# Four graph layers on one core: one table for maximum and sum, a later hold, wide passes in pieces, and a division moved behind the block builder

## The reference, cut to what matters

```python
# first layer: attention over a node's incoming edges
e = leaky_relu(concat(h[src], h[dst], rel[type]) @ attn_w1 @ attn_w2, 0.01)
ex = exp(e - segment_max(e, dst)[dst])
a = ex / segment_sum(ex, dst)[dst]
h_new = where(deg > 0, segment_sum(a * h[src], dst), h); relu(h_new + h @ loop_weight)
# second layer: sum of messages; then two rounds of weighted averaging
# last layer: 8 heads, the edges and a loop at every node
e = a_src[src] + a_dst[dst]; e = where(e > 0, e, 0.2 * e)
e = exp(e - segment_max(e, dst)[dst])
alpha = e / (segment_sum(e, dst)[dst] + 1e-16)
out = segment_sum(alpha * (h @ W_att)[src], dst).mean(heads) + bias
# then two layer norms with a feed-forward block between them
```

## Time and profile before

| | us |
|---|---|
| median of 3 executions | 3177.5 (3170.21 to 3187.55) |
| profiled execution, its own time | 3182.19 |
| its span | 3180.5 |
| busy: TensorE, VectorE, GpSimd, ScalarE | 2093.6, 1963.4, 1061.6, 551.9 |

### The profile page before, as it was taken

How to read it: one execution, slowest core, us unless ns; L and a number is a source line. 1 busy time by engine, 2 the same in 40 slices (tenths; PEclk the granted TensorE clock), 3 DMA queues, 4 the chain that set the end, 5 groups by cost and what they waited for, 6 DMA issues and landing times.

```text
span 3180.5 us, 45724 instructions
## 1 busy us (share of the span) xinstructions
PE 2093.6 (66%) x15154; PEld 1599.8 (50%) x15155; DVE 1963.4 (62%) x3088; ACT 551.9 (17%) x1123; POOL 1061.6 (33%) x984
## 2 busy tenths in 40 slices
PE   0426881699999879979995777774016777614463
PEld 0411221588887779953334666664015666514462
DVE  6789996888898720040104999999935555502274
ACT  0000001344454414410001222221030000000010
POOL 1014002400000000000003777774867777877300
PEclk9655885899999959989997999998558999955575
DMA  2034331233333425548772221220173343212440
GB/s 74 1 80 103 119 100 26 85 144 143 156 161 161 174 95 181 189 176 297 265 289 53 52 52 39 82 52 21 34 252 104 87 124 89 49 25 76 55 88 10
DMA packets 157367, 346.89 MB, mean 109 GB/s; under 512 B 67016, under 2 KB 81523, under 8 KB 150037
## 3 DMA queue, kind: packets, MB, share of 16 engines
q1 hardware_dynamic: 88677, 169.61, 15.8%
q10 hardware_dynamic: 36560, 141.07, 12.5%
q0 software_dynamic: 32032, 34.94, 5.9%
HBM read 220.22 MB, written 124.90 MB: 109 GB/s over the span
## 4 chain that ended last, share of the span: by engine, by line
PE 30%; DVE 24%; POOL 19%; issue 15%; DVEq 3%; DMA 1%; ACT 1%; SPq 0%; POOLq 0%; ACTq 0%
POOL ring L681 16%; PE PS L1226 8%; DVE big L1827 5%; PE PS L1190 4%; PE PS L1261 3%; DVE big L1947 3%; PE PS L1198 2%; PE PS L1251 2%; DVE big L1941 2%; DVE s_ring L1676 2%; PE PS L1073 2%; PE PS L1067 1%; DVE big L1823 1%; DVE s_ring L1670 1%; POOL nmx L687 1%
## 5 line engine op out<-in xcount | busy, mean ns | idle before, releaser
L681 POOL DMA_INDIRECT ring<-d_h,idx_lin x784 | 836.2, 1067 | 848.4 <-DMA d_h<-Hn 557.4
L1306 PEld LDWEIGHTS PS<-arena,s_ring 128*128 128x128 f32 x1968 | 316.1, 212 | 21.9 <-issue 0.4
L1306 PE MATMUL PS<-arena,s_ring 128*128 x1968 | 304.8, 282 | 0.0
L1827 DVE TENSOR_TENSOR big<-big,qa 128x900 bf16<-128x900 bf16 x525 | 296.9, 622 | 0.0
L1122 PE MATMUL PS<-big,qa 128*128 128x225 bf16 x1050 | 262.3, 266 | 38.2 <-DVE big L1827 37.4
L1226 PE MATMUL PS<-big,arena 125*64 125x500 f32 (+1 forms) x700 | 270.4, 546 | 25.8 <-DVEq L1362 25.8
L1999 DVE TENSOR_TENSOR big<-big,PS 128x512 f32 x123 | 84.5, 687 | 321.6 <-PE PS L1306 319.7
L1125 PE MATMUL PS<-big,qa 128*128 128x150 bf16 x2100 | 268.7, 233 | 0.0
L1261 PE MATMUL PS<-big,arena 125*128 125x200 bf16 x2352 | 238.4, 252 | 0.4 <-ACT arena L908 0.4
L1302 PE MATMUL PS<-zero_bf 128*128 128x512 bf16 x123 | 51.0, 415 | 270.8 <-ACTq L949 123.5
L1251 PE MATMUL PS<-big 128*125 128x128 bf16 x784 | 133.0, 293 | 129.5 <-DVE big L1941 125.2
(11 more groups left out here) (446 smaller groups left out, 3629.7 us busy)
## 6 DMA issues: line engine op xcount, KB each, us to landing
big<-d_blk SPq DMA_DIRECT2D x24, 2000.0 KB, 7.6
d_blk<-big ACTq DMA_DIRECT2D x13, 3125.0 KB, 9.2
big<-d_blk SPq DMA_DIRECT2D x25, 1562.5 KB, 6.3
d_blk<-arena ACTq DMA_DIRECT2D x12, 3125.0 KB, 9.2
big<-d_blk SPq DMA_DIRECT2D x12, 2250.0 KB, 8.1
d_stash<-ring SPq DMA_DIRECT2D x98, 256.0 KB, 2.0
arena<-d_stash ACTq DMA_DIRECT2D x98, 256.0 KB, 2.7
ring<-d_h,idx_lin POOLq DMA_INDIRECT x784
```

The costliest lines, as they stand in the source:

```text
L681: pool.indirect_dma_start(ring[:, HALF * h + s, :], None, table, bass.IndirectOffsetOnAxis(ap=idx_lin[:, CH * i + s:CH * i + s + 1], axis= ...
L1306: mm = nc.tensor.matmul(PS[:, bass.ds(place[s] + j % SUMS * BANK, D)], marks[:, j % 2, s, :], arena[:, bass.ds(at[s], D)], start=False, st ...
L1827: last = v_.tensor_tensor(pair_c(half, p, 1, 6, 1), pair_c(half, p, 0, 6, 0), at_wa[:, :, :, bass.ds(k + 2 * p, 2)], ALU.mult)
```

## The change

- **Last layer, one table.** Maximum and sum stand side by side in `big`, 16 values an edge, and are written together to `d_top3`. One group of 25 reads brings both to the nodes (`ntop`), in place of two groups. The column stride of both is 64 bytes. The zeroing of the accumulator stands behind this one write. The write of the maxima ahead of exp is gone.
- **The hold** stands behind 44 chunks (40 before), the alpha rows behind 54 (50).
- **Wide passes** are cut in four pieces each, issued one behind the other.
- **First layer.** The exponentials are written to `d_al0` as they are. The backward fill of the sum, the reciprocal and the product are gone; the forward sums are written to `d_sum0`, and 25 more reads bring them to the nodes (`tot0`, 1 for nodes without edges), behind those of `norm`. Behind the last block, VectorE takes their reciprocal and multiplies `agg_sb` by it. ScalarE's first block waits for the write, since it overwrites the sums.
- Helpers (`col`, `scan_heads`, `row_carry`) now take an array with its stride and offset; `node_terms` and the copies of the escape factors use `ntop`.

```diff
-        FILL_AT, LOOK_AT, ROWS_AT, NODES_AT = 24, 40, 50, 84
+        FILL_AT, LOOK_AT, ROWS_AT, NODES_AT = 24, 44, 54, 84
...
+            sp.wait_ge(S["exp_done"], 1)
+            sp.dma_start(d_al0.rearrange("(p c) k -> p (c k)", p=P), qa[:, 0:C]).then_inc(S["alpha_out"], 16)
             sp.wait_ge(S["alpha_ready"], 1)
-            sp.dma_start(d_al0.rearrange("(p c) k -> p (c k)", p=P), qa[:, 0:C]).then_inc(S["alpha_out"], 16)
+            sp.dma_start(d_sum0.rearrange("(p c) k -> p (c k)", p=P), arena[:, C:2 * C]).then_inc(S["codes_out"], 16)
...
             node_rows(d_wsum, free(norm[:, 0:1], [[1, NB], [1, 1]]), last_i)
+            pool.wait_ge(S["codes_out"], 16 * 8)
+            node_rows(d_sum0, free(tot0[:, 0:1], [[1, NB], [1, 1]]), last_i)
...
-            pool.wait_ge(S["nmx_ready"], 1)
-            pool.wait_ge(S["max_out"], 16)
-            node_rows(d_max3, packed(nmx, H), last_i)
+            pool.wait_ge(S["ntop_ready"], 1)
             pool.wait_ge(S["scan_out"], 16)
-            node_rows(d_sum3, packed(nsum, H), last_i)
+            node_rows(d_top3, ntop, last_i)
             tiles(d_h3, NODES_AT, NCH)
...
             act.wait_ge(S["dense_ready"], 1)
+            act.wait_ge(S["codes_out"], 16 * 8)
             block_out(None, 0, True)
...
             act.wait_ge(S["exp_in"], 2)
-            act.dma_start(d_max3.rearrange("(p c) k -> p (c k)", p=P), big[:, 0:W3]).then_inc(S["max_out"], 16)
             nc.scalar.activation(qa[:, 0:W3], qa[:, 0:W3], ACT.Exp).then_inc(S["exp_done"], 1)
...
             act.wait_ge(S["scan_ready"], 2)
-            act.dma_start(d_sum3.rearrange("(p c) k -> p (c k)", p=P), big[:, W3:2 * W3]).then_inc(S["scan_out"], 16)
-            act.wait_ge(S["max_out"], 16)
-            for j in range(W3 // BANK):
-                nc.scalar.activation(acc[:, j * BANK:(j + 1) * BANK], zero_bf[:], ACT.Copy)
+            act.dma_start(d_top3.rearrange("(p c) k -> p (c k)", p=P), big[:, 0:2 * W3]).then_inc(S["scan_out"], 16)
             act.wait_ge(S["scan_out"], 16)
-            for j in range(W3 // BANK, NB * HD // BANK):
+            for j in range(NB * HD // BANK):
                 last = nc.scalar.activation(acc[:, j * BANK:(j + 1) * BANK], zero_bf[:], ACT.Copy)
...
-            for back in (0, 0, 1, 0, 1):
+            for back in (0, 0, 1, 0):
                 chain(1, back)
...
             go(v_.memset(norm[:], 0.0))
+            go(v_.memset(tot0[:], 1.0))
...
                 scan_one(q, b1, notst, cf_sum, SUMOP, 0.0)
-                scan_one(b1, b2, notst, cb_sum, FILLOP, 0.0, 1)
-                go(v_.reciprocal(b0, b2))
-                go(v_.tensor_tensor(q, q, b0, ALU.mult))
                 mark("alpha_ready")
...
+            def col(b, j):
+
+                return free(b[0][:, 0:1], [[b[1], C]], b[2] + j)
+
+            def wide(b, k):
+
+                return free(b[0][:, 0:1], [[b[1], C // 4], [1, H]], b[2] + k * C // 4 * b[1])
...
-                q, sm, total = qa[:, 0:W3], big[:, 0:W3], big[:, W3:2 * W3]
+                q, sm, total = (qa[:, 0:W3], H, 0), (big[:, 0:2 * W3], 2 * H, 0), (big[:, 0:2 * W3], 2 * H, H)
+
+                def combine(op):
+
+                    for k in range(4):
+                        go(v_.tensor_tensor(wide(q, k), wide(q, k), wide(sm, k), op), False)
+                    v.wait_ge(S["dve"], done[0])
...
-                row_carry(sm, cf_sum, SUMOP, 0.0, 0, lambda: v_.tensor_tensor(q, q, sm, ALU.add))
+                row_carry(sm, cf_sum, SUMOP, 0.0, 0, lambda: combine(ALU.add))
...
-                go(v_.scalar_tensor_tensor(q, q, slope, q, ALU.mult, ALU.max))
+                for k in range(4):
+                    go(v_.scalar_tensor_tensor(wide(q, k), wide(q, k), slope, wide(q, k), ALU.mult, ALU.max), False)
+                v.wait_ge(S["dve"], done[0])
...
-                go(v_.tensor_tensor(q, q, sm, ALU.subtract))
+                combine(ALU.subtract)
                 mark("exp_in")
...
+            v.wait_ge(S["nodes_in"], 16 * NB * 2)
+            go(v_.reciprocal(tot0[:], tot0[:]))
+            go(v_.tensor_tensor(agg_sb[:, 1:NB + 1, :], agg_sb[:, 1:NB + 1, :], bc(tot0[:], D), ALU.mult))
             go(v_.tensor_tensor(T1[:], Hn[:], bc(nfl[:, 3, :], D), ALU.mult))
```

More of the change, by code:

```diff
@@ L958, in _ @@
             act.wait_ge(S["tabs_in"], 64)
-            for g, t in enumerate((nsum, nmx)):
-                ins = nc.scalar.copy(packed(t, NB * H)[0:WH, 0, 0:P].rearrange("p (h t) -> p h t", h=H), free(esc_w[:, 0:1], [[1, H], [H, TW16]], g * P))
+            for g in range(2):
+                ins = nc.scalar.copy(esc_h[:, g * P:(g + 1) * P].rearrange("p (h t) -> p h t", h=H), free(esc_w[:, 0:1], [[1, H], [H, TW16]], g * P))
             ins.then_inc(S["exp_done"], 1)
@@ L1310, in _ @@
             pe.wait_ge(S["exp_done"], 4)
-            for g, t in enumerate((nsum, nmx)):
-                tr = nc.tensor.transpose(bank(6, P, WH, g * WH), packed(t, NB * H)[0:WH, 0, 0:P], ident[0:WH, 0:WH])
+            for g in range(2):
+                tr = nc.tensor.transpose(bank(6, P, WH, g * WH), esc_h[:, g * P:(g + 1) * P], ident[0:WH, 0:WH])
             tr.then_inc(S["esc_tr"], 1)
@@ L1742, in row_carry, with scan_heads @@
                 chains[0] += 1
[L1744 removed]
+            def scan_heads(to, vals, flags, cf, ops, neutral, mask, fix, back=0):
                 for j in range(H):
[L1747 to L1748 removed]
+                    go(v_.tensor_tensor_scan(heads(to[0], to[2] + j, to[1], back), heads(flags, 0, 1, back), heads(vals[0], vals[2] + j, vals[1], back), neutral, *ops), False)
+                row_carry(to, cf, ops, neutral, back)
                 for j in range(H):
[L1750 removed]
+                    go(v_.scalar_tensor_tensor(col(to, j), mask, carry[:, j:j + 1], col(to, j), *fix), False)
                 v.wait_ge(S["dve"], done[0])
             def softmax3(slope):
[L1755 removed]
+                q, sm, total = (qa[:, 0:W3], H, 0), (big[:, 0:2 * W3], 2 * H, 0), (big[:, 0:2 * W3], 2 * H, H)
[3 more added lines that the diff above has]
+                    v.wait_ge(S["dve"], done[0])
                 v.wait_ge(S["fill_in"], 16 * 3)
@@ L1758, in softmax3 @@
                     for j in range(H):
-                        go(v_.tensor_tensor_scan(free(sm[:, 0:1], [[H, C2]], h * C2 * H + j), notst[:, h * C2:(h + 1) * C2], free(fa_half[h][:, 0:1], [[H, C2]], j),
-                                                 sm[:, (C2 - 1) * H + j:(C2 - 1) * H + j + 1] if h else 0.0, *SUMOP), False)
+                        last = free(big[:, 0:1], [[1, 1]], (C2 - 1) * 2 * H + j)
+                        go(v_.tensor_tensor_scan(free(big[:, 0:1], [[2 * H, C2]], h * C2 * 2 * H + j), notst[:, h * C2:(h + 1) * C2], free(fa_half[h][:, 0:1], [[H, C2]], j),
+                                                 last if h else 0.0, *SUMOP), False)
                     v.wait_ge(S["dve"], done[0])
-                row_carry(sm, cf_sum, SUMOP, 0.0, 0, lambda: v_.tensor_tensor(q, q, sm, ALU.add))
+                row_carry(sm, cf_sum, SUMOP, 0.0, 0, lambda: combine(ALU.add))
                 for j in range(H):
-                    go(v_.scalar_tensor_tensor(col(q, j, H), first_m, carry[:, j:j + 1], col(q, j, H), ALU.mult, ALU.add), False)
+                    go(v_.scalar_tensor_tensor(col(q, j), first_m, carry[:, j:j + 1], col(q, j), ALU.mult, ALU.add), False)
                 v.wait_ge(S["dve"], done[0])
-                go(v_.scalar_tensor_tensor(q, q, slope, q, ALU.mult, ALU.max))
+                for k in range(4):
+                    go(v_.scalar_tensor_tensor(wide(q, k), wide(q, k), slope, wide(q, k), ALU.mult, ALU.max), False)
+                v.wait_ge(S["dve"], done[0])
                 scan_heads(sm, q, negst[:, 0:C], cf_max, MAXOP, -BIG, first_neg, MAXOP)
@@ L1776, in node_terms @@
             def node_terms():
-                top, shift = free(asd[:, 0, 0:1], [[1, NB * H]]), free(asd[:, 0, 0:1], [[1, NB * H]], NB * H)
-                found, own, total = (free(t[:, 0, 0:1], [[1, NB * H]]) for t in (nmx, nself, nsum))
+                top, shift = asd[:, :, 0:H], asd[:, :, H:2 * H]
+                found, own, total = ntop[:, :, 0:H], packed(nself, H), ntop[:, :, H:2 * H]
                 v.wait_ge(S["nodes_in"], 16 * NB * 3)
@@ L1923, in _ @@
             mark("asd_sb")
[L1924 to L1926 removed]
+            go(v_.memset(ntop[:, :, 0:H], -BIG))
+            go(v_.memset(ntop[:, :, H:2 * H], 0.0))
+            mark("ntop_ready")
             go(v_.tensor_copy(iota_look.rearrange("p (c s) -> p c s", s=CB), free(iota_row[:, 0:1], [[1, W], [0, CB]])))
```

33 lines of the change are left out of this document (14 added, 19 removed).

## The result

The changed kernel takes 3080.6 us (median of four runs, 3080.07 to 3083.33) where the kernel before takes 3175.6 beside it: a ratio of 0.970, with a 95% interval of 0.967 to 0.973. The forecast of 3078 was 2.6 us off. The profiled execution has a span of 3078.7 us against 3180.5, 101.8 less, where the sum said 100.

What follows compares the result with a forecast made beforehand. GpSimd's queue was taken to set the end from the look-up on; terms -41 - 36 - 12 + 0 + 0 + 2 - 13 = -100 us from a median of 3177.5 gave 3078 us, range 3057 to 3120.

Steps and rivals of the forecast that it cites:

- What bounds: From 2200 to 2985 us the end follows GpSimd's queue; a microsecond taken from it is one taken from the kernel.
- Node reads, -41: Last layer: 25 of 50 node reads on GpSimd go, 41 us saved, bounds -39 and -42.
- Hold, -36: GpSimd in the look-up: four more chunks remove its 36.0 us pause, 36 us saved, bounds 0 and -36.
- Pieces, -12: Last layer's softmax: four gathers pass where one did, 9 more in three passes, 12 us saved, bounds 0 and -13.
- Side by side, 0: Last layer's columns 64 bytes apart instead of 32 cost VectorE nothing more; other bound +37 us.
- Write and zeroing, 0: Softmax end: doubled write takes 20 us, first step 10 to 20 later but covered; 0, bounds -4 and +10.
- First layer, -13: Dense blocks start 15 us earlier, reciprocal and product cost 2 behind the builder, 25 extra reads nothing; net -13 us.
- Catch-up, +2: Last layer's steps:, last gather near 2890 instead of 2976.5, -87 where the terms give -89: +2 us.
- Columns did not get dearer: Rival on the last layer's wider columns: 37 us more on VectorE and as much on GpSimd, 3115 us; chance 0.10.
- The step loop did not take over: Rival on the last layer's step loop: steps take 4.69 us throughout instead of 3.58, kernel 3137 us; chance 0.08.
- The gap between pieces: Rival on the softmax pieces: no gap, back-to-back VectorE instructions keep GpSimd out, 3090 us; chance 0.07.
- The rival that the hold protects the look-up: Rival in the look-up: 32 gathers lengthen it by what they save, kernel 3114 us; chance 0.05.

Runs made afterwards that it cites:

- the experiment: Under First layer: changed kernel with first layer as before, 3949.2 us, second kind of chip; under The rivals: changed kernel with hold behind 40 chunks, 3122.9 us, first kind.
- the run early: Changed kernel with the last layer's node terms at step 104 instead of 116: 3064.9 us on the first kind of chip, 3952.8 on the second.
- the second run of whole passes: Changed kernel with the last layer's add, slope and subtract as one pass each again, repeated; second kind of chip, 3960.0 us.

## Why the prediction was right

**What bounds.** That GpSimd's queue sets the end from the look-up on was right, on the chips for which the prediction was made: the last gather came 99.7 us earlier and the end 101.8. That the sum met it within 2 us is in part luck: the node reads gave 2 less than their term and the first layer some 3 less, while 1.9 us that were there before the change's first instruction and 2.1 us less behind the last gather stood in no term.

**Node reads, -41.** Measured: two groups of 83.4 us became one of 44.5, that is -38.9. The row length is not what sets the price: reads of 64 bytes averaged 1477 ns here and 1268 to 1307 on the second kind of chip, reads of 32 bytes 1370 and 1264, reads of 4 bytes 1476 and 1680. The sum took the dearer estimate.

**Hold, -36.** The pause is gone (-36.0), the look-up pays nothing back, and undoing it alone costs about 41 us, 35.5 of it the pause.

**Pieces, -12.** Right: three gathers of 6.4 to 7.0 us are replaced by four of 1.4 to 1.7 each. VectorE pays 0.2 us a pass, 6.89 against 6.69.

**Side by side, 0.** Right in the sum, wrong in the parts. VectorE gets eight 64-byte columns 0.66 us cheaper (11.71 against 12.37). Its softmax up to the exponentials takes 104.7 us instead of 107.1: 1.3 less for two such passes, 0.6 more for the pieces, and 1.7 less because the exponentials start sooner behind the subtract (VectorE waits 5.58 us for them instead of 7.26). Nobody foresaw that part. In the kernel before, ScalarE first issued the write of the maxima and then loaded the table of its exponential, 1.28 us:

```profile
2305.40 0.35 ACTq L921 DMA_DIRECT2D d_max<-big  x1
2305.78 1.28 ACT L922 ACT_TABLE_LOAD   x1 [110.59 <-DVEq L1362]
2307.07 5.43 ACT L922 ACTIVATE qa<-qa 128x6272 f32<-128x6272 f32 x1
```

With that write gone, the load comes 103 us ahead of the exponentials:

```profile
2190.32 1.28 ACT L926 ACT_TABLE_LOAD   x1 [6.22 <-issue]
2293.56 5.43 ACT L926 ACTIVATE qa<-qa 128x6272 f32<-128x6272 f32 x1 [101.96 <-DVEq L1363]
```

GpSimd loses 4 to 13 us in seven of the nine traces to gathers that miss their boundaries, 4.4 in the profiled one. The bound of +37 was far off: the price steps up between 8 and 16 bytes and falls a little at 64.

**Write and zeroing, 0.** The write took 19.2 us against the 20 forecast. Counted from the end of the look-up, the first step comes 4.3 us later (206.6 against 202.3), not 10 to 20: the softmax is 2.4 us shorter, and of the 9.4 us that the write grew by only 6.7 lay open. GpSimd waits 4.1 us for the stash where it waited 4.4. That a large write stops GpSimd was priced at up to +10 and is real: four of them cost it 47 us, on the second kind of chip.

**First layer, -13.** The start of the dense blocks moved 14.3 us against the scan that hands over the exponentials (48.8 against 63.1), 14.9 in the experiment, with -15 predicted. GpSimd's 16 gathers took 27.9 us from the first to the last end instead of 24.8: +3.1 where +2 was said. Reciprocal and product took 0.32 and 1.83. Behind the builder the gain is 12.2 us by the clock of the trace (1097.03 against 1109.27); 1.9 of them were there before the change's first instruction, since the scan came at 511.85 instead of 513.74. So the change gave 10.3 in this pair of traces, 7.4 to 10.4 over the four traces of the changed first layer on this kind of chip, and 10 to 14 in the experiment. The term of 13 was set a little too high, most of it in the builder, which took 534.1 to 537.2 us in these four where 532.5 had been counted on.

**Catch-up, +2.** Chunk 84 was to come near 2693, the reads to end at 2736, the last gather at 2890. The reads ended at 2724 and the last gather came at 2876.76; with the 11.1 us of the first layers, which the hand forecast left out, added again, that is 2735 and 2888.

**The rivals.** Columns did not get dearer. The step loop did not take over: a few steps behind the start took 4.7 us and the later ones about 3.6. The gap between pieces exists. The rival that the hold protects the look-up is false on the chips of the forecast, by the experiment, and true on the other kind.

## Two kinds of chips

This was not expected and is the largest effect seen, some 810 us for the same program. No chip on record came up a second time, so "kind of chip" is a reading: a state that a chip is in for a time would look the same. Up to the last layer the kinds agree (with the new first layer, the first gather of the last one starts between 1701 and 1715 us in all traces). Then, while GpSimd gathers, the loops of the other engines crawl: when GpSimd reached its hold at 2209, 10 of the look-up's 196 groups were done in the run early. The run early on the second kind, VectorE in the look-up:

```profile
1819.70 0.99 DVE L1969 TENSOR_TENSOR big<-PS,qa 128x800 f32<-128x800 f32 x1 [42.25 <-issue]
1820.83 0.98 DVE L1975 TENSOR_REDUCE qa<-big 128x800 f32 x1
1821.73 0.42 DVE L1963 TENSOR_TENSOR big<-big,gone 128x512 bf16<-128x512 bf16 x1
1864.59 0.99 DVE L1969 TENSOR_TENSOR big<-PS,qa 128x800 f32<-128x800 f32 x1 [42.44 <-remote]
```

Once GpSimd stops at its hold, a group takes 2.36 us there too, as on the first kind (VectorE of the run with the old first layer):

```profile
2619.06 0.98 DVE L1962 TENSOR_TENSOR big<-PS,qa 128x800 f32<-128x800 f32 x1
...
2621.42 0.98 DVE L1962 TENSOR_TENSOR big<-PS,qa 128x800 f32<-128x800 f32 x1
```

GpSimd then waits 466 us for the look-up, and the first step comes at 2926 to 3069 instead of 2396. The waits are put down to nothing on the core ("issue", "remote"), most of them 32 to 55 us long, on TensorE, ScalarE and VectorE alike, so it is not TensorE's loops alone, as the expectation of the second run of whole passes had it. They come about once a turn of the loop. What they wait for stays open and wasn't tried apart. That the engines wait for their instructions while gathers are under way is a guess: the DMA packets that the profile marks "instruction" number 98 on both kinds, and only three of them fall into those ten groups. For the change it suggests that its worth hangs on the chip: hold, reads and pieces buy GpSimd's time, and there this time seems to be bought from the other engines. The kernels with one part undone or added ran there at 0.988 to 0.998 of the kernel before; the change itself wasn't timed there.

## What to carry over

When one engine's queue sets the end, its instructions are the sum: fewer of them, no pause, and shorter neighbours on VectorE, each worth its own length until the next engine is late. Find that next one in the same trace; here it was an exponential queued behind the last reload, and moving it gave another 12 to 17 us.

Where gathers wait beside a long VectorE pass, try pieces a little longer than one gather; of the sizes tried here these let most gathers through. And know on which chip a trace was taken before its waits are trusted elsewhere.
